# Second weight layer of a graph attention kernel: from three rounded passes over 512 columns to fp32 products over two column halves

## The reference, cut to what matters

```python
def tensor_product(x_e, sh, w, C):            # w: [E,128] weights of each edge
    acc = sh[:, 0:1] * (x_e @ C[:, 0, :])
    for s in range(1, 9):
        acc = acc + sh[:, s:s + 1] * (x_e @ C[:, s, :])
    return acc * w

def mlp2(x, w1, b1, w2, b2):
    return jax.nn.relu(x @ w1 + b1) @ w2 + b2

wk = mlp2(edge_features, k_w1, k_b1, k_w2, k_b2)
wv = mlp2(edge_features, v_w1, v_b1, v_w2, v_b2)
k = tensor_product(x_dst, edge_sh, wk, Cqk).reshape(-1, H, DQK)
v = tensor_product(x_dst, edge_sh, wv, Cv).reshape(-1, H, DV)
attn = jnp.einsum('ehd,ehd->eh', q[edge_src], k)
... softmax over the edges of a node, weighted sum of v, projection, norms
```

## Time and profile before

| | us | share of the span |
|---|---|---|
| median of 3 runs | 3005.49 | |
| profiled execution, its own time | 3001.06 | |
| its span | 2999.2 | 100% |
| TensorE busy | 2506.8 | 84% |
| VectorE busy | 2631.2 | 88% |
| ScalarE busy | 1531.1 | 51% |
| GpSimd busy | 1778.8 | 59% |

### The profile page before, as it was taken

How to read it: one execution, slowest core, us unless ns; L and a number is a source line. 1 busy time by engine, 2 the same in 40 slices (tenths; PEclk the granted TensorE clock), 3 DMA queues, 4 the chain that set the end, 5 groups by cost and what they waited for, 6 DMA issues and landing times.

```text
span 2999.2 us, 48368 instructions
## 1 busy us (share of the span) xinstructions
PE 2506.8 (84%) x12505; PEld 1789.6 (60%) x12505; DVE 2631.2 (88%) x3781; ACT 1531.1 (51%) x2914; POOL 1778.8 (59%) x1719
## 2 busy tenths in 40 slices
PE   2233357999999999999999999999999999999714
PEld 1232325667776766777667776777667776776511
DVE  6688736899999998999999999999899999999737
ACT  1321234556656665566566565566566666666310
POOL 2700027777777776777677776777677777776030
PEclk7555557999999999999999999999999999999855
DMA  6786713344444444444444444444444444444340
GB/s 183 208 228 183 195 40 91 87 127 148 143 142 145 143 139 136 141 144 140 136 138 141 146 141 137 141 143 142 136 138 141 145 141 138 147 144 128 108 135 11
DMA packets 282404, 415.29 MB, mean 138 GB/s; under 512 B 64463, under 2 KB 191875, under 8 KB 278470
## 3 DMA queue, kind: packets, MB, share of 16 engines
q1 hardware_dynamic: 222278, 296.67, 31.5%
q0 software_dynamic: 52704, 107.19, 13.9%
q10 hardware_dynamic: 7128, 8.13, 0.8%
HBM read 309.59 MB, written 102.20 MB: 137 GB/s over the span
## 4 chain that ended last, share of the span: by engine, by line
PE 55%; DVE 21%; issue 9%; DMA 6%; ACT 4%; SPq 2%; POOL 1%; DVEq 1%; POOLq 0%; ACTq 0%
PE bank L1117 12%; PE bank L1119 10%; PE bank L1118 10%; PE bank L1162 5%; PE bank L1141 5%; DVE run_c L1429 4%; DVE xa_t L1537 4%; DMA keep_c<-keep_d 3%; DVE z_l L1545 3%; ACT z_h L875 2%; PE bank L1124 2%; PE bank L1123 2%; PE bank L1193 2%; DVE val L1574 2%; PE bank L1112 2%
## 5 line engine op out<-in xcount | busy, mean ns | idle before, releaser
L744 POOL DMA_INDIRECT gathered<-xtab_d,src_g x784 | 831.9, 1061 | 448.8 <-PE bank L1094 191.8
L744 POOL DMA_INDIRECT gathered<-qtab_d,dst_g x784 | 810.0, 1033 | 256.0 <-issue 250.7
L1117 PE MATMUL bank<-z_h,wt_h 128*128 128x512 f32 x1568 | 745.5, 475 | 51.8 <-DVE val L1574 49.1
L875 ACT ACTIVATE z_h<-xa_t 128x512 fp32r<-128x512 f32 x980 | 620.5, 633 | 289.1 <-DVE xa_t L1537 176.5
L1537 DVE TENSOR_TENSOR xa_t<-bank,r_r 128x512 f32<-128x512 f32 x980 | 662.8, 682 | 3.7 <-PE bank L1141 1.2
L1119 PE MATMUL bank<-z_h,wt_l 128*128 128x512 f32 x1568 | 621.0, 396 | 0.0
L1118 PE MATMUL bank<-z_l,wt_h 128*128 128x512 f32 x1568 | 620.2, 396 | 0.0
L1545 DVE TENSOR_TENSOR z_l<-xa_t,z_h 128x512 fp32r<-128x512 f32 x784 | 536.1, 684 | 85.8 <-ACT z_h L875 70.1
L1117 PEld LDWEIGHTS bank<-z_h,wt_h 128*128 128x128 f32 x1568 | 302.0, 193 | 112.7 <-issue 71.9
L1141 PE MATMUL bank<-s,sel 128*128 128x512 bf16 x980 | 349.5, 389 | 2.6 <-DVE xa_t L1537 2.1
L1119 PEld LDWEIGHTS bank<-z_h,wt_l 128*128 128x128 f32 x1568 | 295.0, 188 | 71.6
(11 more groups left out here) (222 smaller groups left out, 3952.8 us busy)
## 6 DMA issues: line engine op xcount, KB each, us to landing
nrow_d<-x_r SPq DMA_DIRECT2D x196, 288.0 KB
ea<-in_ea_t SPq DMA_DIRECT2D x392, 128.0 KB
exb<-exd_d SPq DMA_DIRECT2D x392, 128.0 KB
dmb<-exd_d SPq DMA_DIRECT2D x392, 128.0 KB
ea_c<-in_ea_t SPq DMA_DIRECT2D x49, 512.0 KB, 5.0
aggrow_d<-xa_t SPq DMA_DIRECT2D x49, 512.0 KB, 3.8
gathered<-xtab_d,src_g POOLq DMA_INDIRECT x784
gathered<-qtab_d,dst_g POOLq DMA_INDIRECT x784
```

Source lines behind the costliest of these rows:

```text
L744: rows_in = pool.indirect_dma_start(rows[:, c % 4, k, :], None, table, bass.IndirectOffsetOnAxis(ap=picked[:, s, at:at + 1], axis=0))
L875: act.activation(z_h[:, c % 2, i, :], z[:, i, :], ACT.Copy).then_inc(zh_ok, 1)
L1117: pe.matmul(ps[:, :], wt_h[rows, w, :], high, start=start, stop=False)
```

## The change

`weights` no longer uses `split_matmul`. The second layer's weights stay unsplit in a tile `w2kv` of their own (keys' weights on partitions 0 to 63, values' on 64 to 127). The fp32 `hid` is multiplied with them in fp32, 256 columns at a time, and keys and values alternate. `hid_h`, `hid_l`, the step `hidden_low` and its semaphore are gone, and the split tiles of the weights have 11 slots in place of 12.

```diff
-CK, CV, W2KV, W1KV = 0, NJ, 2 * NJ, 2 * NJ + 1
-NW = 2 * NJ + 2
+CK, CV, W1KV = 0, NJ, 2 * NJ
+NW = 2 * NJ + 1
...
+        w2kv = sb("w2kv", [P, O])
...
-                   (wt[0:D, W2KV, :], a["k_w2"]), (wt[D:P, W2KV, :], a["v_w2"]),
+                   (w2kv[0:D, :], a["k_w2"]), (w2kv[D:P, :], a["v_w2"]),
...
                 act.activation(hid[:, :], ps_hw[:, :], ACT.Relu, bias=b1kv[:, :]).then_inc(hid_ok, 1)
-                act.activation(hid_h[:, :], ps_hw[:, :], ACT.Relu, bias=b1kv[:, :]).then_inc(hid_ok, 1)
...
             def weights(j, c):
-                done(pe, hidl_ok, j, c)
+                done(pe, hid_ok, j, c)
...
-                for ps, rows, done_ps in ((ps_xw, slice(0, D), wk_ps), (ps_hw, slice(D, P), wv_ps)):
-                    split_matmul(ps, W2KV, hid_h[rows, :], hid_l[rows, :], True, True, rows).then_inc(done_ps, 1)
+                for f in range(2):
+                    edges = slice(f * HG, (f + 1) * HG)
+                    mk = pe.matmul(ps_xw[:, edges], w2kv[0:D, :], hid[0:D, edges], start=True, stop=True)
+                    mv = pe.matmul(ps_hw[:, edges], w2kv[D:P, :], hid[D:P, edges], start=True, stop=True)
+                mk.then_inc(wk_ps, 1)
+                mv.then_inc(wv_ps, 1)
...
-            def hidden_low(j, c):
-
-                done(dve, hid_ok, j, c, 2)
-                past(dve, wv_ps, j, c, 1)
-                dve.tensor_tensor(hid_l[:, :], hid[:, :], hid_h[:, :].bitcast(F32), ALU.subtract
-                                  ).then_inc(hidl_ok, 1)
...
                     outer(j, c + 1, 1)
-                    hidden_low(j, c + 1)
                     outer_low(j, c + 1, 0)
```

More of the change, by code:

```diff
@@ L227, in gnn_two_layers @@
         hid = sb("hid", [P, G])
-        hid_h = sb("hid_h", [P, G], F32R)
-        hid_l = sb("hid_l", [P, G], F32R)
         qt = sb("qt", [P, 2, G])
@@ L397, in gnn_two_layers @@
         zl_ok = sem("zl_ok")
-        hidl_ok = sem("hidl_ok")
         wth_ok = sem("wth_ok")
```

## The result

The changed kernel took 3020.3 us (median of 5 runs, 3017.57 to 3025.51), the kernel before 3003.34 us beside it (2995.71 to 3006.69). The ratio is 1.006 with a 95% interval of 1.0041 to 1.0078: slower by 17 us. That is inside the stated range (2995 to 3090) and of the forecast sign, but 18 us under the 3038 that was said, at the low end of the forecast's own range (3018 to 3062). The profiled execution took 3018.45 us over a span of 3016.5, against 3001.06 and 2999.2.

A forecast was written before the change was run, and what follows sets the result against it. TensorE was taken to bound the plain bodies; seven bodies paying 0.22 us less 0.30 us gained gave +1.24 us a batch, +35 us over 28 batches, forecast 3038 us. The stated range was 2995 to 3090.

The forecast's parts named there:

- TensorE is the chain of the plain bodies: In the plain bodies of a batch TensorE is busy for all 11.42 us and sets the time.
- The passes pair over the two halves of the rows: In `weights`, eight fp32 passes run as four pairs on upper and lower 64 rows, 1.13 us against 0.91.
- staggered: Rival: fp32 passes in `weights` keep strict order, five steps, 0.45 us more than before, 3081 us; chance 0.10.
- serial rival: Rival: fp32 passes in `weights` do not overlap, eight steps, 1.14 us more than before, 3216 us; chance 0.05.
- The price of a pair: In `weights`, two fp32 passes together take 0.23 us (0.21 to 0.26), so each body pays 0.22 us more.
- VectorE's release is worth 0.30 us in seven bodies: The dropped 0.60 us subtraction gains 0.15 us in the first and second body each, nothing in the others.
- The rival in which it counts in the batch bodies: Rival: the first body drops to 12.15 us, the second to 11.64; 2998 to 3015 us, no change; chance 0.15.
- The first and second body: Batch bodies of 12.75 and 11.75 us: each pays 0.22 us for `weights` and gains 0.15 before `z_h` 2.
- The third body: Body of 13.28 us: gains nothing from VectorE and pays 0.22 us, since `batch_turn` stands behind `weights`.
- ScalarE's activation, counted at nothing: One ScalarE activation fewer at the head of each body, where ScalarE has room; counted at nothing.
- VectorE as the bound: Rival: VectorE sets every body's time, so each group is 0.60 us shorter, 2883 us; chance 0.10.
- the 130 of the sign: Expected in the profile: VectorE's busy time falls by about 130 us (196 records of 0.68) while the time does not.

The follow-up runs named there:

- the reordered kernel: The changed kernel with its four fp32 instructions in the order keys, keys, values, values instead of alternating: 3019.52 us, ratio 1.0073 to the kernel before.
- `z_h` 2 first: ScalarE's `outer_high` 2 moved ahead of `batch_turned` and `weights_v`: 2968.41 us from the changed kernel, 2961.34 from the kernel before, 2946.99 from the latter without the subtraction.

## Why the prediction was right, point by point

- **TensorE is the chain of the plain bodies.** Held: the chain has only matmuls in both kernels, and doubling the products lengthened each body by all of 4 x 0.216 us.
- **The passes pair over the two halves of the rows.** Held, and in both orders that were run. The staggered and the serial rival, 3081 and 3216 us, fell with the pairs in the trace and with the reordered kernel.
- **The price of a pair.** This term was mis-sized. It was put at 0.23 us between ends of 0.21 and 0.26; it is 0.216, near the low end. So `weights` costs 0.15 us more, not 0.22. With that value the sum reads 7 x 0.15 - 0.30 = +0.75 us, which is what the batch shows (+0.74), and +21 us instead of +35. The step from 21 to the measured 17 us is in the jump bodies, for which the sum had no term; that it falls on this side was luck, as far as the runs show.
- **VectorE's release is worth 0.30 us in seven bodies.** Held beside the old products: taking the subtraction out of the kernel before gave 0.16 + 0.19 = 0.35 us. Beside the new ones it is worth 0.06. The rival in which it counts in the batch bodies is wrong while `z_h` 2 stands behind `wv`, and right once it does not (0.54 us per batch). Its condition, that `z_h` 2 does not hold the first body, was not met in either kernel.
- **The first and second body.** The net held: 12.75 stays, and 11.75 becomes 11.72. The prediction books it as 0.15 us paid and 0.15 us gained, but they are one and the same 0.15 us: `z_h` 2 had it to spare behind `wv`, and either the longer `weights` takes it up or the release gives it back. With the subtraction put back these two bodies did not grow either.
- **The third body.** Held: +0.15 us, through `batch_turn`.
- **ScalarE's activation, counted at nothing.** No run takes it out alone. In the kernel before without the subtraction it already makes VectorE wait, but for less than the 0.45 us that are over before `outer_low` 2, so it costs nothing there; with `z_h` 2 first it does (12.51 us against 12.15 expected).
- **VectorE as the bound** (2883 us). Fell: its 196 subtractions were added for 2 us, as the batches show it. Its busy time fell by 109 us, not by the 130 of the sign (196 records of 0.68): the records overlap, and start 0.60 us apart.

The net is a trade of the scarcer engine's time for the other's: a fourth pair on TensorE in every body, which five of seven pay, against a subtraction for which VectorE had room or time to wait.

## What to carry to other kernels

Work taken off an engine is worth only what the next wait leaves of it; follow the freed engine to its next wait and ask which engine that one's releaser waits for. Here a single step in ScalarE's order, put ahead of two steps that wait for TensorE, took 1.3% off the kernel before and 1.7% off the changed one, and the product itself moved 0.6%. Price a change of precision in passes: here an fp32 product of 512 columns is four passes of 256 at 0.216 us, together 0.86 us, and three rounded passes of 512 columns at 0.23 are 0.69. And read the room of an engine from the starts of its instructions, not from its busy time.

## What the runs showed of the hardware that was not expected

- A pair of fp32 passes of 256 columns takes 0.216 us from start to start, while a pair of rounded passes of 512 columns takes 0.23, with weight loads of 0.186 us before both. So the weight load alone does not set the step of 0.23; what does was not tried.
- TensorE starts passes on different halves of its rows together also when the two instructions of one half stand ahead of the other's (four passes of keys, then four of values), in 1.07 us against 1.06 with alternation.
- A GpSimd subtraction of 128x512 takes 1.28 us. A VectorE scan over two SBUF inputs takes 1222 ns, and 2663 where the two overlap; an operation with one input in PSUM keeps its 684.
- In the bodies in which the loop jumps back, TensorE stands idle for 1.1 to 3.6 us. The granted clock falls in some of them and not in others: 0.89 after 2.5 us in the kernel before, 1.00 after 2.8 in the changed one. In the kernel before such a body takes 15.8 us where the clock is 0.89 and 13.8 where it is 1.00.
